# Fused feed-forward, attention and feed-forward block: the table of row numbers is requested from GpSimd's queue and no longer from SyncE's

## The reference

```
logits = x @ gate_w.T;  probs = softmax(logits);  topk_w, topk_ids = top_k(probs, 2)
topk_w = topk_w / sum(topk_w)
buf = zeros(64, 257, 256).at[se, pos_c].set(x[tok])      # rows of each expert, in their places
gu = einsum('ech,ehf->ecf', buf[:, :256], w13);  g, u = split(gu)
yb = einsum('eci,eih->ech', silu(g) * u, w2)
moe_out = zeros(T, 256).at[tok].add(w_slot * yb[se, pos_c])
out = (moe_out + shared).reshape(B, S, 256) + residual
```

## Time and profile before

| what | value |
|---|---|
| median of 3 runs | 2043.13 us (2042.89 to 2043.6) |
| span of the profiled execution, first to last instruction | 2040.7 us |
| TensorE busy | 1945.9 us, 95% of the span |
| VectorE, ScalarE, GpSimd busy | 1305.8, 1093.1, 1102.2 us |
| mean granted TensorE clock | 0.982 |

### The profile page before, as it was taken

One profiled execution on the slowest core, in us unless ns is written; L12 is line 12 of the kernel. 1 busy time (PEld: TensorE's weight loads), 2 busy tenths in 40 slices (PEclk: granted clock), 3 DMA queues, 4 the chain that ended last, 5 costly groups with the idle time before them and its releaser, 6 DMA issues.

```text
span 2040.7 us, 32594 instructions
## 1 busy us (share of the span) xinstructions
PE 1945.9 (95%) x11074; PEld 1661.1 (81%) x11074; DVE 1305.8 (64%) x3481; ACT 1093.1 (54%) x1988; POOL 1102.2 (54%) x1262
## 2 busy tenths in 40 slices
PE   6997999699999999999999999999999996899998
PEld 4776999578888888888888888888888886599975
DVE  5996677456557576575665765756657545466659
ACT  6873777334545455454454544544545534577775
POOL 5664777442364555645546456455552532577753
PEclk9998999899999999999999999999999998899998
DMA  8544999790022032120320311102100040499969
GB/s 278 183 158 135 323 325 323 227 278 22 13 92 83 22 104 60 45 88 16 104 83 22 104 29 34 42 21 62 42 22 24 19 132 9 93 343 328 397 234 333
DMA packets 234295, 267.99 MB, mean 131 GB/s; under 512 B 25425, under 2 KB 184210, under 8 KB 234130
## 3 DMA queue, kind: packets, MB, share of 16 engines
q1 hardware_dynamic: 205458, 198.69, 29.9%
q0 software_dynamic: 28672, 67.22, 9.7%
HBM read 149.31 MB, written 116.52 MB: 130 GB/s over the span
## 4 chain that ended last, share of the span: by engine, by line
PE 67%; DVE 8%; issue 3%; ACT 2%; POOL 1%; DMA 1%; DVEq 0%; SPq 0%; ACTq 0%; POOLq 0%
PE attention_ring L2133 23%; PE attention_acc L2163 14%; PE attention_acc L2153 9%; PE attention_acc L2403 3%; PE attention_ring L2391 2%; PE attention_acc L2391 2%; PE attention_work L2209 2%; DVE attention_hid L1815 2%; PE attention_work L2226 2%; PE attention_work L2242 2%; PE attention_work L2246 2%; PE attention_ring L2378 1%; PE attention_work L2121 1%; PE attention_work L2183 1%; ACT attention_xn L1443 1%
## 5 line engine op out<-in xcount | busy, mean ns | idle before, releaser
L1815 DVE TENSOR_TENSOR attention_hid<-attention_gelu,attention_hid 128x512 fp32r<-128x512 f32 x384 | 286.7, 747 | 487.7 <-ACT attention_gelu L1433 318.2
L1430 ACT ACTIVATE attention_hid<-attention_ring,home_b 128x512 fp32r<-128x512 f32 x384 | 264.3, 688 | 533.7 <-PE attention_ring L2133 533.2
L2163 PE MATMUL attention_acc<-attention_hid,home_w_h 128*128 128x512 f32 x1024 | 361.2, 391 | 3.1 <-DVE home_room L1832 1.7
L1433 ACT ACTIVATE attention_gelu<-attention_ring,home_b 128x512 f32<-128x512 f32 x384 | 261.6, 681 | 0.0
L2163 PEld LDWEIGHTS attention_acc<-attention_hid,home_w_h 128*128 128x128 f32 x1024 | 192.2, 188 | 49.3 <-DVE home_room L1832 9.4
L2133 PE MATMUL attention_ring<-attention_n_t_h,home_w_h 128*128 128x512 f32 x512 | 203.9, 398 | 1.6 <-DVE attention_n_t_l L1807 1.6
L2153 PE MATMUL attention_acc<-home_w_h,attention_hid 128*128 128x256 f32 x1024 | 204.4, 283 | 0.0
L2133 PE MATMUL attention_ring<-attention_n_t_h,home_w_l 128*128 128x512 f32 x512 | 199.8, 390 | 0.0
L2133 PE MATMUL attention_ring<-attention_n_t_l,home_w_h 128*128 128x512 f32 x512 | 199.5, 390 | 0.0
L2163 PE MATMUL attention_acc<-attention_hid,home_w_l 128*128 128x512 f32 x512 | 199.3, 389 | 0.0
L1260 POOL DMA_INDIRECT home_room<-expert_rows,routing_slots x128 | 136.5, 1066 | 91.6 <-DVE home_room L1646 38.1
(11 more groups left out here) (330 smaller groups left out, 4819.3 us busy)
## 6 DMA issues: line engine op xcount, KB each, us to landing
early_w<-in_L_ffn_w SPq DMA_DIRECT2D x64, 256.0 KB, 4.7
expert_rows<-experts_y SPq DMA_DIRECT2D x64, 256.0 KB, 4.0
slot_rows<-const_zeros SPq DMA_DIRECT2D x16, 1024.0 KB, 10.3
token_rows<-const_zeros SPq DMA_DIRECT2D x16, 1024.0 KB, 10.0
home_room<-in_L_ffn_w SPq DMA_DIRECT2D x64, 256.0 KB, 4.8
final_y_rows<-token_rows SPq DMA_DIRECT2D x32, 512.0 KB, 7.7
dispatch_x_in<-in_L_attn_x SPq DMA_DIRECT2D x16, 512.0 KB, 6.7
xn_rows<-dispatch_xn SPq DMA_DIRECT2D x16, 512.0 KB, 4.2
```

The lines of the kernel that those rows point to most:

```text
L1430: act.activation(hid[n % PARTS][0][:, :], ring[n % RING][:, :], ACT.Gelu, bias=b1[:, m, c:c + 1])
L1433: act.activation(gelu[n % GELUS][:, :], ring[n % RING][:, :], ACT.Gelu, bias=b1[:, m, c:c + 1]).then_inc(ring_free, 1)
L1815: dve.tensor_tensor(hid[n % PARTS][1][:, :], gelu[n % GELUS][:, :], hid[n % PARTS][0][:, :].bitcast(fp32), ALU.subtract).then_inc(hid_read ...
L2163: last = pe.matmul(acc[e % 3][:, :], w2[m][wp][:, c, k * P:(k + 1) * P], hid[s][xp][:, :], start=(c == 0 and q == 0), stop=(c == FC - 1 an ...
```

## The change

SyncE no longer waits for the number scatters and no longer loads `who`. GpSimd does both, right behind its own last number scatter and ahead of the wait for the load's landing. The semaphore `who_loaded` is now one of those kept for GpSimd's DMAs.

```
-        who_loaded, slots_turned, xe_rounded, xe_split = sem("who_loaded"), sem("slots_turned"), sem("xe_rounded"), sem("xe_split")
+        who_loaded, slots_turned, xe_rounded, xe_split = sem("who_loaded", gathers=True), sem("slots_turned"), sem("xe_rounded"), sem("xe_split")
...
             for e in range(YR, EXPERTS + 3):
...
-                if e == YR + 1:
-                    for h in (HALVES - 2, HALVES - 1):
-                        sp.wait_ge(*scattered(meta_scattered, h))
-                    sp.dma_start(who, meta_d[0:SLOTS, :].rearrange("(p e c) a -> p e (c a)", p=P, c=CH)).then_inc(who_loaded, 16)
...
             scatter_meta(last - 1, 7, 8)
             scatter_meta(last)
+            for h in (HALVES - 2, HALVES - 1):
+                pool.wait_ge(*scattered(meta_scattered, h))
+            pool.dma_start(who, meta_d[0:SLOTS, :].rearrange("(p e c) a -> p e (c a)", p=P, c=CH)).then_inc(who_loaded, 16)
             pool.wait_ge(who_loaded, 16)
             for e in range(EXPERTS):
                 pool.wait_ge(y_copied, e + 1)
```

## The result

| kernel | median us | ratio to before, 95% interval |
|---|---|---|
| before | 2043.18 (21 runs) | |
| changed | 2046.12 (21 runs) | 1.0012 [1.0007, 1.0018] |
| changed, once more (e7) | 2045.06 (11 runs) | 1.0013 [1.0004, 1.0022] |

The ratio of 1.0012 is 2.5 us. The change made the kernel slower by more than its measurement is uncertain, and by less than the 0.2% that I had called no change. Each comparison has its own runs of the kernel before beside it: their median was 2043.18 us here and 2043.05 for e7. By the medians the loss is 2.9 us here and 2.0 for e7. Two single runs that took far longer, one of e12 at 4707.93 us and one of the kernel before beside e11 and e12 at 2492.45 us, are left out of every median and ratio.

What follows compares the result with a forecast made beforehand. GpSimd's last scatter was taken to set the last stage's start. Freed SyncE queue 0, two waits 0, load 1.3 us later lifting the lag one step, +1.27 us: median from 2043.13 to 2044.4 us, range 2042.6 to 2047.2.

Steps and rivals of the forecast that it cites:

- one step: GpSimd's lag behind the copies rises one rung, to 4.39 us; last scatter and end come 1.27 us later.
- rival 2: SyncE's unpaused loads in the queues slow GpSimd's load to 5.0 to 7.1 us; 2045.7 to 2046.9 us; chance 0.28.
- No change: Whole kernel's time changes by under 0.2%, 4.1 us; chance 0.85.
- What bounds the kernel: End of the experts: GpSimd's last result scatter sets the last stage's start, microsecond for microsecond.
- SyncE's freed queue, 0: SyncE's loads from expert 10 on, up to 7.8 us earlier, gain nothing; losing the cover costs nothing.
- The two waits on GpSimd, 0: GpSimd, idle from 1772.97 to 1788.84, takes SyncE's waits for the number scatters at no cost.
- The load, 1.3 us later: GpSimd's load of `who` lands after 4.7 us, not 3.4, so the first scatter starts 1.3 us late.
- What VectorE's L2042 would add to the load: VectorE's two-input instruction, L2043 before, may hold GpSimd's load at its request: up to 0.4 us more.
- The lag and its steps: GpSimd's scatters lock to VectorE's L2043 at set lags behind the copies; each step adds 1.26 or 1.27 us.
- Rival 1: GpSimd's load lands as fast as SyncE's; time 2043.1 us, or 2042.8 if level with the last copy; chance 0.2.
- Rival 3: First direct GpSimd load needs over 7.7 us from the wait's end; over 4.1 us slower; chance 0.12.
- Rival 4: Freed SyncE loads remove TensorE's 1.3 us stall near 1787; change worth 2043.1 us; chance 0.05, with other speedups over 0.3 us.

Runs made afterwards that it cites:

- e7: The changed kernel timed and profiled once more, against the kernel before: 2045.06 us, ratio 1.0013.
- e12: Changed kernel, SyncE's loads from expert 8 on held until `who` landed, TensorE's first last-stage product moved behind the last expert's second product: 2042.21 us, ratio 0.9994.
- e11: Changed kernel, but behind expert 9's loads SyncE waits until `who` has landed: 2044.46 us, ratio 1.0006.
- e2: Kernel before with one unused 128x256 add on GpSimd ahead of its first scatter: 2045.19 us, ratio 1.0008.
- e4: Kernel before, but SyncE requests `who` ahead of the loads of experts 8 and 9: 2043.26 us, ratio 1.0.
- e9: Changed kernel, but SyncE requests nothing of experts 8 and on until `who` has landed: 2043.37 us, ratio 1.0.
- e1: Changed kernel, but SyncE also waits for the number scatters at its old place, without its load of `who`: 2045.2 us, ratio 1.0008.
- e5: Kernel before with VectorE's L2043 over 16 of 256 columns: 2042.46 us, ratio 0.9997.
- e6: Changed kernel with VectorE's same instruction over 16 of 256 columns: 2043.84 us, ratio 1.0003.
- e8: Kernel before, SyncE requesting `who` ahead of experts 8 and 9, TensorE's first last-stage product behind the last expert's second product: 2040.49 us, ratio 0.9986.
- e10: Kernel before with TensorE's first last-stage product moved behind the last expert's second product, nothing else: 2043.53 us, ratio 1.0001.
- e3: Kernel before with three unused 128x256 adds on GpSimd ahead of its first scatter: 2045.2 us, ratio 1.001.

## Why the prediction was right, point by point

The time fell into the range, but not by the way of the forecast (one step, chance 0.35): the load was slow for the reason of rival 2 (0.28), and 2046.12 lies in rival 2's figures. "No change" by the stated 0.2%, at 0.85, was right.

**What bounds the kernel.** The place was right. A later start of GpSimd against the copies went with a higher lag and a later last scatter. "Microsecond for microsecond" was too strong for one execution, since the last stage by itself varied by 2.3 us (78.4 to 80.7).

**SyncE's freed queue, 0.** Right as a gain: the loads came earlier, and the last copy stands 175.7 us behind expert 0's in the changed kernel as in e2 to e4 with the old order. Wrong as "the price of the cover going is nil". The freed loads run beside GpSimd's load and make it 2.2 us slower (e11 against e7). I had this as a reason for rival 2 and not as a term.

**The two waits on GpSimd, 0.** Half right: behind them stood nothing that was hurt. But from the landing to the request it took GpSimd 0.58 us, in e7 and e9 too, where SyncE took 0.06: 0.5 us that I had not priced.

**The load, 1.3 us later.** This is the term that was too small. From the landing of the numbers to the first scatter I had 0.06 + 4.7 + 0.25 = 5.0 us, and it was 6.30 in the changed kernel and 6.27 in e7. Of the miss of 1.3 us, 0.5 is the later request above, and 0.7 to 0.8 is the landing: I took the gathers' median of 4.7 us, and it was 5.35 to 5.45 in four profiles. Against 3.71 before, the change costs 2.6 us there. In the two profiles 0.8 and 1.6 us of it are hidden, since the numbers landed that much earlier, by chance. It is luck, therefore, that e7's first scatter (1789.75) and last (1963.83) stand so near the forecast's 1790.14 and 1963.6.

**What VectorE's L2042 would add to the load.** Nothing, as far as it was seen. In the changed kernel L2042 did not run at the request (1783.84 to 1784.52, then from 1786.12; the request at 1784.95), nor in e7 or e9. In e1 it did:

```profile
1787.67 0.69 DVE L2045 TENSOR_TENSOR attention_n_t_l<-home_room,attention_n_t_h 128x512 fp32r<-128x512 f32 x1
...
1788.01 0.59 POOL L1397 DMA_DIRECT2D attention_gelu<-slot_ids  x1 [11.62 <-DMA slot_ids<-attention_row_id,attention_meta_at]
```

The request took the same 0.59 us and landed after 5.36, as elsewhere. So the direct load was not held, by this one meeting, where the indirect ones are. The rule that I had set against the change holds for the scatters and did not show on the load. I had also stretched it. The box in the Trainium skill, "SBUF — State Buffer", speaks of VectorE instructions in a mode with two ports, and the list above it, in the same section on the two separate sides, sets one with two SBUF inputs only against a GpSimd instruction that reads SBUF. The scatters read their row numbers there; the direct load has none to read.

**The lag and its steps.** Right, and that L2043 holds the lag is shown by e5 and e6. Of the ladder 1.62, 3.12, 4.39, 5.89, 7.15, worked out from the earlier trace rows, the profiles have 1.61, 3.12, 5.88 and 7.14, and e8 has the one below, 0.36. 4.39 did not come up at expert 30: no profile without the stall and with the full L2043 has a first scatter between 3.72 and 5.80 us behind expert 0's copy, and e10 stood at 4.39 at expert 1 and left it when the stall came. One count was off: from 1945.80 on there are 14 scatters, not 13. And a step down brings 0.1 us, not 0.3, since a scatter starts 0.27 us behind its copy at best (e4, e9).

**The sum.** The forecast was one step, +1.3 us, 2044.4; measured were +2.5 us and 2046.12, inside the stated 2042.6 to 2047.2. Two steps of lag, as in rival 2, are what e7's profile shows (5.88), with the stall gone; the last scatter itself came one step later. The reason of rival 2 (the unpaused loads of SyncE in the queues) is what e9 and e11 show. How 2.6 us of delay become 2.5 in the median is argued and not shown: against expert 0's copy the start varies by more than a step between executions (2.0 to 5.1 us with SyncE's load in its old place and the adds left aside, 3.1 to 5.8 in the changed kernel, e7 and e6), so the steps should average to about the delay; these profiles are too few to show it. The 2.4 us that I added for what lies outside the span were too many: it is 1.7 to 1.8 us in every run here, and the kernel before was profiled in an execution somewhat faster than its median. The difference does not hang on it.

**What would show it.** Of the signs of being right, the request's time came (1784.95 and 1784.06). Expert 10's rows were requested before 1782 in e7 alone. The lag of 4.39 did not come, and the scatter of 1.20 us was the second of its pair in both profiles. The lag of 5.89 was my sign that the load is slower than I took it.

**Rival 1** (as quick as SyncE's) is out, unless the queues are kept clear, as in e9. **Rival 3** (a dear first GpSimd load) is out: from the end of the wait to the landing it was 6.0 us, not over 7.7, and 2.0 us from the request alone; nor did the number scatters land later (10.7 to 12.0 us after the last one's issue in the changed kernel, e7 and e6, 13.1 before). **Rival 4**, the nameless stall of TensorE: it is gone from both profiles of the changed kernel, but also from e2, e3 and e5, which have SyncE's old list. It comes and goes between executions. In time nothing was seen of it, but the lag of a profile can't be read without it, as e7 shows.

## What to carry to other kernels

A wait in an engine's request list can be a shield: it holds back the loads behind it while a small load that others wait for runs. Before it is removed, ask what the freed requests will run beside. A small load on a path that matters lands soonest in queues that are empty, from whichever engine, though here that brought the time of before and not less (e4, e9). A follower that seems to have slack (2.52 us of work in 2.77) may never use it when another engine's instruction catches it once a turn: read the lag at several places of the stage, not the rates. And take more than one profile where a change is worth a microsecond or two: the executions of one kernel differed here by more than that.

## What the runs showed of the hardware

- The landing of a 64 KB load from GpSimd was 2.0 us in empty queues, 3.2 beside loads already queued, and 5.4 beside SyncE's running loads; it came out at 5.35 to 5.45 in four executions. SyncE's own, ahead of its burst, was 1.9 in empty queues (e4, e8) and 2.5 to 4.0 with loads queued (five executions).
- GpSimd's scatters lock to one VectorE instruction with two SBUF operands (0.69 us) at discrete lags. With that instruction at 0.19 us there is no lock. The box in the Trainium skill, "SBUF — State Buffer" (section on the two separate sides), blames instructions in a mode with two ports; the list above it and "GPSIMD Engine Reference", Key points, name two SBUF inputs too, and this trace agrees with these: a held scatter took 1.20 us and a free one 0.96.
- A direct load on GpSimd started 0.58 us behind the landing that it waited for, on SyncE 0.06 us.
- TensorE's granted clock fell from 2.4 to 1.2 GHz for a few microseconds in the last stage of the four profiles with a lag of 5.88 or more, behind a stretch in which it was mostly idle.
- 128x256 adds in bf16 on GpSimd took 0.61 to 1.09 us.
- The last of 9 scatters of 4-byte numbers in a row, issued 1.26 us apart, landed 9.7 to 13.3 us after its issue. When the first expert's rows were requested varied by 4.5 us between profiles whose instructions up to there are the same.
